# Attention on one Trainium2 core: the residual add and its statistics move from the end of a turn into the first step of the next turn

## The reference

```
x = _layernorm(x + _L0_attn_ref(x, Wq, bq, Wk, bk, Wv, bv, Wo, bo), axis=-1)

Q = (x @ Wq + bq).reshape(b, s, KV, G, DH)      # KV = 4, G = 4, DH = 128
K = (x @ Wk + bk).reshape(b, s, KV, DH)
V = (x @ Wv + bv).reshape(b, s, KV, DH)
attn = softmax(einsum('bqkgd,bpkd->bkgqp', Q, K) * scale)
out = einsum('bkgqp,bpkd->bqkgd', attn, V).reshape(b, s, H * DH)
return out @ Wo + bo
```

## Time and profile before

| | us |
|---|---|
| median of three runs | 1016.36 |
| the three runs | 1014.90 to 1017.05 |
| profiled execution, first to last instruction | 1014.8 |
| in it, self-attention | about 391 |
| one turn of the loop | 45.8 |

### The profile page before, as it was taken

The page is one execution under the profiler, slowest core; times in us unless marked ns, Lnnn a source line. Parts: engine busy times, 40 slices in busy tenths (PEclk is TensorE's granted clock), DMA queues, the critical chain, the costliest instruction groups (busy, mean ns, idle before and its releaser), DMA issues. The chain is left out here.

```text
span 1014.8 us, 15713 instructions
## 1 busy us (share of the span) xinstructions
PE 938.7 (93%) x5588; PEld 779.6 (77%) x5588; DVE 666.2 (66%) x1315; ACT 518.9 (51%) x1218; POOL 373.9 (37%) x252
## 2 busy tenths in 40 slices
PE   6899999999999997877798889999999999999993
PEld 5799999999999986756687657777777777777772
DVE  4656565555556564567578767676767776777675
ACT  4556465565556462144343365555555555555543
POOL 1622121222122120344234245555555555555431
PEclk9999999999999998899788989999999999999997
DMA  6300000000000003000100212020202020200002
GB/s 217 98 1 22 5 16 10 10 10 10 21 0 10 1 11 128 1 0 1 61 6 6 72 39 81 22 81 22 81 21 81 21 80 21 80 21 21 22 1 83
DMA packets 16428, 37.97 MB, mean 37 GB/s; under 512 B 2048, under 2 KB 6912, under 8 KB 15232
## 3 DMA queue, kind: packets, MB, share of 16 engines
q1 hardware_dynamic: 15744, 35.29, 10.5%
q0 software_dynamic: 640, 2.10, 0.6%
HBM read 34.76 MB, written 2.62 MB: 37 GB/s over the span
## 5 line engine op out<-in xcount | busy, mean ns | idle before, releaser
L234 POOL TENSOR_TENSOR att_probs<-att_probs,att_share 128x512 f32<-128x512 f32 x64 | 66.4, 1039 | 191.8 <-DVE att_share L517 191.8
L1459 POOL TENSOR_TENSOR all_xT_hi<-moe_xe,all_xT_hi 128x1024 fp32r<-128x1024 f32 x31 | 79.2, 2556 | 104.9 <-ACT all_xT_hi L1598 104.8
L1467 POOL TENSOR_TENSOR all_xT_lo<-moe_inner,all_xT_lo 128x512 fp32r<-128x512 f32 x64 | 84.5, 1321 | 88.7 <-ACT all_xT_lo L1637 86.8
L421 ACT ACTIVATE att_probs<-att_score,att_bias 128x128 f32<-128x128 f32 x256 | 90.7, 381 | 41.8 <-DVE att_bias L508 41.7
L1707 DVE TENSOR_TENSOR moe_inner<-moe_gu,moe_silu 128x512 f32<-128x512 f32 x64 | 43.9, 686 | 81.6 <-ACT moe_silu L1633 63.5
L1637 ACT ACTIVATE all_xT_lo<-moe_inner 128x512 fp32r<-128x512 f32 x64 | 40.3, 630 | 100.2 <-DVE moe_inner L1707 100.2
L554 DVE SCALAR_TENSOR_TENSOR att_OT_lo<-att_mix,att_bv,att_OT_hi 128x512 fp32r<-128x512 f32 x64 | 45.9, 750 | 58.4 <-ACT att_OT_hi L459 58.4
L459 ACT ACTIVATE att_OT_hi<-att_mix,att_bv 128x512 fp32r<-128x512 f32 x64 | 43.5, 704 | 66.1 <-PE att_mix L50 66.1
L48 PE MATMUL att_proj<-att_xT_hi,att_Wq_hi 128*128 128x256 f32 x256 | 74.8, 292 | 1.7 <-DVE att_Wq_lo L482 0.9
L48 PE MATMUL att_acc<-att_Wo_hi,att_OT_hi 128*128 128x256 f32 x256 | 73.0, 285 | 1.6 <-DVE att_OT_lo L554 1.6
L50 PE MATMUL att_proj<-att_xT_hi,att_Wq_lo 128*128 128x256 f32 x256 | 72.1, 282 | 0.0
(11 more groups left out here) (298 smaller groups left out, 2934.9 us busy)
## 6 DMA issues: line engine op xcount, KB each, us to landing
all_stage<-in_expert_w SPq DMA_DIRECT2D x8, 1152.0 KB, 5.8
moe_spread<-soft_dram SPq DMA_DIRECT2D x64, 128.0 KB
all_scale<-in_expert_scale SPq DMA_DIRECT2D x8, 320.0 KB, 6.8
att_xT<-in_xT SPq DMA_DIRECT2D x8, 256.0 KB, 3.1
att_stage<-in_Wq SPq DMA_DIRECT2D x4, 512.0 KB, 7.6
att_stage<-in_Wo SPq DMA_DIRECT2D x4, 512.0 KB, 5.6
att_x_tok<-in_x_tok POOLq DMA_DIRECT2D x8, 256.0 KB, 3.1
out<-all_r SPq DMA_DIRECT2D x4, 512.0 KB, 4.4
```

What stands on the lines that cost most here:

```text
L234: pool.tensor_tensor(p3, p3, each, ALU.mult).then_inc(prob_ready, 1)
L421: ins = act.activation(p_[:, c], score[b][:, c], ACT.Exp, bias=bias[b][:, h:h + 1], scale=SCALE, accum_out=m_[:, h:h + 1])
L1459: pool.tensor_tensor(xe[u % 2].lo[:, :], xe32[:, :], xe[u % 2].hi[:, :].bitcast(F32), ALU.subtract).then_inc(xe_lo, 1)
L1467: pool.tensor_tensor(innerT[u % 2].lo[at], inner[at], innerT[u % 2].hi[at].bitcast(F32), ALU.subtract).then_inc(inner_lo, 1)
```

## The change

The end of a turn (L560 to L571) is cut in two functions, `add_input` and `keep`, and both are called inside step 0 of the next turn: the add behind the two `low_p` and ahead of the shares, the statistics and the two copies behind the projected queries and ahead of `OT_lo`. The wait for the copies moves to the end of the turn that made them. Turn 0, which has nothing to add, is taken out of VectorE's loop and written out; for the last turn both calls stand behind it, as before. The queues of the other engines have the same instructions in the same order.

```diff
-            def turn(g, last):
+            def add_input(g):
+                dve.wait_ge(acc_ready, g + 1)
+                dve.wait_ge(xb_ready, g + 1)
+                dve.tensor_tensor(r_now[:, :], acc[:, :], x_tok[:, :], ALU.add).then_inc(r_ready, 1)
+
+            def keep(g):
+                dve.wait_ge(r_ready, g + 1)
+                for b in range(PAIR):
+                    ins = dve.bn_stats(stats[:, 6 * b:6 * b + 6], r_now[:, b * D:(b + 1) * D])
+                ins.then_inc(stats_ready, 1)
+                dve.tensor_scalar(r1[:, bass.ds(g * PAIR * D, PAIR * D)], r_now[:, :], 1.0, None, ALU.mult
+                                  ).then_inc(kept_ready, 1)
+                dve.wait_ge(stats_ready, g + 1)
+                dve.tensor_scalar(stats1[:, bass.ds(g * PAIR * 6, PAIR * 6)], stats[:, :], 1.0, None, ALU.mult
+                                  ).then_inc(kept_ready, 1)
+
+            def turn(g, first, last):
...
                     if j in TURNED_FIRST:
                         for b in range(PAIR):
                             low_p(g, j, b)
+                    if j == 0 and not first:
+                        add_input(g - 1)
                     for b in range(PAIR):
                         if ahead:
                             shares(g, j + 1, b)
...
                     for what in step_units(j, last):
                         n += 1
                         unit_part(what, g, n)
+                    if j == 0 and not first:
+                        keep(g - 1)
...
-            with dve.Fori(0, TURNS - 1) as g:
-                turn(g, False)
-            turn(TURNS - 1, True)
+            turn(0, True, False)
+            with dve.Fori(1, TURNS - 1) as g:
+                turn(g, False, False)
+                dve.wait_ge(kept_ready, 2 * g)
+            turn(TURNS - 1, False, True)
+            dve.wait_ge(kept_ready, 2 * TURNS - 2)
+            add_input(TURNS - 1)
+            keep(TURNS - 1)
+            dve.wait_ge(kept_ready, 2 * TURNS)
```

## The result

The changed kernel takes 1018.7 us against 1016.1 us for the kernel before (medians of 17 runs each). The ratio is 1.0028, with a 95% interval of 1.0020 to 1.0035: 2.8 us slower. The forecast was 1018.1 us with a range of 1015.2 to 1020.2.

The account below looks back on a forecast made before the run. TensorE bounds the kernel, busy 43.99 of 44.70 us a turn. The V product 0.28 us later in six turns, the scores' 0.13 gain used up, adds 1.7 us to the 1016.36 median: 1018.1, range 1015.2 to 1020.2.

Parts of the forecast that it names:

- Where the wait comes from: Scores of step 2: queries follow the second share, which waits for ScalarE; earlier bias gains 0.13 us, 0.51 of 0.64 stays.
- The add at no cost: Step 0, ahead of the shares: the 0.69 us add runs while ScalarE does exponentials, costing nothing, 1.4 us to spare.
- GpSimd's load and products: Load moves with the add, from 125.19 to 129.25; step 1's products queue behind it, 129.85 to 131.89, nothing lost there.
- The statistics: Behind step 0's queries, ahead of OT_lo: start at 130.65, copy of r_now 0.67 later; with undisturbed copies OT_lo 0.56 us late.
- The slower rival: bn_stats also held by GpSimd's products until 131.89: V product 0.95 us late, 5.7 us slower, 1022.1; chance 0.09.
- The held copy: Copy of r_now meets GpSimd's second product, ends 0.15 us behind it, 0.31 longer; OT_lo 0.87 us later; chance 0.60.
- The longer of the two bounds: Copy of r_now: its whole 0.41 us follows GpSimd's product, 0.26 us more in a turn than forecast.
- The V product: First V product of step 1: OT_lo's 0.87 us lateness exceeds the 0.65 us cover less 0.06; starts 0.28 us later.
- My end for a free copy: Copy not held up: OT_lo's 0.56 us lateness puts the V product 0.03 earlier, -0.2 us in all, 1016.2; chance 0.25.
- the hand-over: From the lo part's end on VectorE to TensorE's V product of step 1: some 0.06 us, taken off the 0.65 cover.
- the upper end, 3.2: Copy's whole 0.41 us behind GpSimd's product: 6 x 0.54 = 3.2 us slower, 1019.6.
- the 2.03 us that I called the same: Whole kernel: 0.2% of the measurement, about what can be told from no change; the same got 0.61, slower 0.33.

Follow-up runs that it names:

- the last runs: Queries between step 0's exponentials: alone on the changed kernel 1.0036; plus probability parts first and statistics in step 1, 0.9929; kernel before with both swaps 0.9933.
- the run with the queries first: Changed kernel with only the projected queries put between the first and second exponentials and shares in step 0: 1.0036 of before, 46.30 us a turn.
- two runs with a free copy: Changed kernel with GpSimd's load behind step 1's products (1.0011 of before), and changed kernel with the add at the turn's end again (1.0011).
- two such swaps: Queries between step 0's exponentials, probability parts ahead of x's in step 1: on kernel before 0.9933; on the changed kernel with statistics in step 1, 0.9929.

## Why the prediction was right, and where it was short

**Where the wait comes from** was right: the queries wait behind the second share, that for ScalarE, and the end of the turn is only one of two things that bind ScalarE. The exponentials start 0.97 us behind the hi parts (124.56 to 125.53), the wait stays at 0.49 us; 0.98 had been read from turn 7, and 0.51 worked out from it. That the queries' place is what holds the scores is shown by the last runs, in which that wait disappears.

**The add at no cost** was right: the share behind it still waits 1.22 us for ScalarE, and the run with statistics and copies in step 1 has the full 0.14 us a turn.

**GpSimd's load and products** came as worked out: the load 0.91 us behind the add (127.07 to 127.98), the products right behind it.

**The statistics** are not held by GpSimd: 0.74 us for the two in the middle of its products. The slower rival is out. Its price had a slip besides: 1.0 us behind 131.89 is 132.9 and not 132.7, which makes 6.7 us instead of 5.7. The Trainium skill's statement (SBUF — State Buffer, "Who interferes with whom") that one SBUF input outside the two-port modes doesn't contend agrees with this row.

**The held copy** was right in kind and place, and too small. The step that mis-sized it is the tail: I took 0.15 us behind the end of GpSimd's product, from an operation of 128x256; here it is 0.30 (130.62 to 130.92), and 0.29 in the run with the queries first (132.18 to 132.47). The longer of the two bounds, the copy's whole 0.41 behind the product, was too much. From the start of the queries to OT_lo it is 2.32 us (128.59 to 130.91) instead of 2.20: 0.12 us of the difference.

**The V product** was right in place and cover, but a price was missing: TensorE doesn't start a waited-for product at its full rate. Its first two matmuls stand 0.34 us apart instead of 0.23, 0.11 us for each turn. The trace of before had it already, in turn 7, which waits there:

```profile
376.93 0.50 PE L48 MATMUL att_mix<-att_PT_hi,att_V_hi 128*128 128x512 f32 x1 [0.81 <-DVE att_PT_lo L512]
377.26 0.40 PE L49 MATMUL att_mix<-att_PT_lo,att_V_hi 128*128 128x512 f32 x1
```

My end for a free copy (-0.2 us in all, -0.03 a turn) was wrong as well: two runs with a free copy came out 0.10 and 0.14 us a turn above the kernel before. About 0.1 us of this miss is the slow beginning; another 0.07 to 0.08 lie in steps 2 and 3, unexplained.

So for a turn: 0.28 forecast, plus 0.12 for the tail and 0.11 for the beginning, less 0.02 for the gain at the scores (0.15, not 0.13) and 0.02 for the hand-over (0.04, not 0.06), is 0.47; measured 0.47. The sum of 1.7 us was 2.8. It lay inside its ends, in part by luck: the upper end, 3.2, was worked out from a longer tail alone and had no price for the slow beginning. And it lay on the other side of the 2.03 us that I called the same: "no change" had the larger chance, and slower is what came. (The 1.56 us between the profiled span and the median is not a faster execution: every run here is timed 1.6 to 1.7 us above its own span. The forecast stays the same by it.)

## What to carry to other kernels

Before moving work off one engine's late spot, look for the second cause that ends at the same time: here two ended within 0.03 us of each other, and the trace named only one. Follow what the moved work releases: an add moved by 4 us (from 0.20 us behind the start of the scores of step 1 to 4.25) moved a load on another engine, and with it a product into the path of a copy. And where an engine that sets the time waits for a result, look at the order in which its helpers make that result first; two such swaps gained 0.87 us a turn, where the best place for the turn's end gained 0.14.

## What the runs showed of the hardware

A tensor_scalar from SBUF to SBUF on VectorE is held while GpSimd runs a product of SBUF operands, and ends about 0.3 us behind it for 128x512 f32 (0.28 to 0.30 in the loop turns of three kernels, the operation alone 0.41). bn_stats from SBUF isn't held (0.74 us for two, 0.76 before). The Trainium skill (SBUF — State Buffer, "Who interferes with whom") has the one that comes second fully block; read to the letter, its whole 0.41 us would follow the other's end, and the traces here have it some 0.1 us shorter. Beside GpSimd's issue of a load (130.50 to 131.08) the same copy took 0.47 us instead of 0.41 (0.47 or 0.48 in the six loop turns; in turn 7 the copy kept its 0.41, and the load's issue took 0.83 us instead of 0.58).

What I hadn't expected is that TensorE loses time on a lateness that its list of waits doesn't show: 0.06 us late (8.51 against 8.45, in the run with the add at the end), no idle time listed, and 0.1 us more until the second matmul. What makes the beginning slower no run shows.
